# Keys and values of two groups projected by one 512-column pass, over three PSUM banks

## The reference

```python
q = rms_norm((ln(x) @ Wq.T).reshape(B, 64, 16, 128)); q = rope(q, itok)
kv_in = concat([ctx, ln(x)], axis=1)
k = rope(rms_norm(kv_in @ Wk.T), pos);  v = kv_in @ Wv.T          # 4 key/value heads, 4 queries each
x = x + tanh(g_xattn) * (softmax(q k^T / sqrt(128)) v) @ Wo.T
y = ln(x)
top = top_k(softmax(y @ w_router), 2)                            # 8 experts
x = x + tanh(g_ffn) * (2.5 * routed(y, top) + shared(y))
```

## Time and profile before

| | |
|---|---|
| median of 3 runs | 1232.29 us (1231.39 to 1232.36) |
| the profiled execution, its own time | 1230.35 us |
| its span | 1228.5 us |
| busy in the span | PE 1201.1, PEld 1115.2, DVE 1036.2, POOL 938.4, ACT 903.3 us |
| MATMUL records of `keys_values`, 256 wide | 1488 |
| MATMUL records of `queries`, 512 wide | 744 |

### The profile page before, as it was taken

How to read it: one execution, slowest core, us unless ns; L and a number is a source line. 1 busy time by engine, 2 the same in 40 slices (tenths; PEclk the granted TensorE clock), 3 DMA queues, 4 the chain that set the end, 5 groups by cost and what they waited for, 6 DMA issues and landing times.

```text
span 1228.5 us, 31467 instructions
## 1 busy us (share of the span) xinstructions
PE 1201.1 (98%) x8765; PEld 1115.2 (91%) x8766; DVE 1036.2 (84%) x3014; ACT 903.3 (74%) x3774; POOL 938.4 (76%) x1124
## 2 busy tenths in 40 slices
PE   6899999999999999999999999999999999999899
PEld 3788999999999999999999999999999899999787
DVE  8788999999999999999999999988888677777434
ACT  7978788878887888788887888877777546666322
POOL 2788888888888888888888888888887425556664
PEclk9999999999999999999999999999999999999989
DMA  6634233322222223323333333222236536554575
GB/s 179 198 110 130 75 108 107 103 90 90 90 90 90 94 90 94 90 90 98 115 106 98 103 107 119 93 76 75 75 110 215 192 101 188 167 163 146 155 250 170
DMA packets 141079, 148.55 MB, mean 121 GB/s; under 512 B 13824, under 2 KB 124672, under 8 KB 140256
## 3 DMA queue, kind: packets, MB, share of 16 engines
q1 hardware_dynamic: 134544, 130.16, 35.1%
q0 software_dynamic: 6480, 17.77, 3.9%
HBM read 66.93 MB, written 80.76 MB: 120 GB/s over the span
## 4 chain that ended last, share of the span: by engine, by line
PE 92%; DVE 4%; ACT 3%; DMA 1%; issue 1%; SPq 0%; DVEq 0%; ACTq 0%
PE b_kv L1795 14%; PE b_q L1781 13%; PE b_o L1879 13%; PE b_sc L1853 9%; PE b_aT L1868 9%; PE b_pT L1861 5%; PE b_qT L1842 4%; PE b_q L2115 3%; PE b_kv L2115 3%; PE b_kT L1838 2%; PE b_q L2175 1%; PE b_kT L2175 1%; PE b_o L2175 1%; PE b_kv L2175 1%; PE b_aT L2132 1%; PE b_pT L2132 1%
## 5 line engine op out<-in xcount | busy, mean ns | idle before, releaser
L1795 PE MATMUL b_kv<-w_group,kv_in_hi 128*128 128x256 f32 x992 | 205.0, 305 | 0.0
L778 POOL TENSOR_TENSOR q_rot<-q_rot,q_sin 128x512 f32<-128x512 f32 x128 | 176.6, 1380 | 7.3 <-DVE q_sin L1327 2.4
L984 ACT ACTIVATE probs<-b_sc,neg_max 128x128 f32<-128x128 f32 x512 | 180.2, 369 | 2.5 <-DVE neg_max L1337 2.1
L774 POOL TENSOR_TENSOR qk_r<-qk_me,minus_half 128x6 f32<-128x6 f32 x128 | 171.8, 1342 | 10.1
L1795 PEld LDWEIGHTS b_kv<-w_group,kv_in_hi 128*128 128x128 f32 x992 | 161.4, 190 | 7.3 <-issue 0.4
L1781 PE MATMUL b_q<-w_group,kv_in_hi 128*128 128x512 f32 x496 | 164.8, 413 | 0.4 <-DVE q_sin L1327 0.4
L1879 PE MATMUL b_o<-wo_hi,aT_hi 128*128 128x256 f32 x480 | 143.6, 299 | 0.3 <-DVE aT_lo L1351 0.3
L1853 PE MATMUL b_sc<-kT,qT 128*128 128x128 f32 x1024 | 136.4, 276 | 6.1 <-ACT qT L973 4.4
L781 POOL TENSOR_TENSOR q_rot<-q_rot,qk_r 128x512 f32<-128x512 f32 x128 | 133.5, 1043 | 10.0
L1795 PE MATMUL b_kv<-w_group,kv_in_lo 128*128 128x256 f32 x496 | 139.7, 282 | 0.0
L1868 PE MATMUL b_aT<-pT,v 128*128 128x256 f32 x512 | 133.9, 384 | 0.0
(11 more groups left out here) (332 smaller groups left out, 3978.2 us busy)
## 6 DMA issues: line engine op xcount, KB each, us to landing
xs_scratch<-zeros SPq DMA_DIRECT2D x34, 1032.0 KB, 6.2
s_in<-xs_scratch SPq DMA_DIRECT2D x71, 129.0 KB, 2.2
yT_scratch<-yT SPq DMA_DIRECT2D x32, 256.0 KB, 2.0
yS<-yT_scratch SPq DMA_DIRECT2D x32, 256.0 KB, 4.1
routed<-ys_scratch SPq DMA_DIRECT2D x32, 256.0 KB, 4.1
w_hi_all<-w_scratch SPq DMA_DIRECT2D x3, 1536.0 KB, 12.7
x_in<-in_x SPq DMA_DIRECT2D x32, 128.0 KB, 2.4
ctx_raw<-in_ctxT SPq DMA_DIRECT2D x32, 128.0 KB, 2.6
```

What stands on the lines that cost most here:

```text
L774: nc.gpsimd.tensor_tensor(qk_r[g % 2][:], qk_me[:], minus_half[:, 0:REP + NB], ALU.pow).then_inc(r_ready, 1)
L778: nc.gpsimd.tensor_tensor(q_rot[g % 2][:], q_rot[g % 2][:], q_sin[g % 2][:], ALU.add) \
L984: last = nc.scalar.activation(probs[:, j, :], b_sc[:, j * P:(j + 1) * P], ACT.Exp, bias=neg_max[g % 2][:, j:j + 1], accum_out=row_sum[g % ...
L1795: last = nc.tensor.matmul(b_kv[:, s * 2 * HD:(s + 1) * 2 * HD], kv_in[p][a][:, c, 2 * s:2 * s + 2, :], wkv_of(b, c)[:, g % KVH, :], start= ...
```

## The change

`b_kv` becomes one tensor of three banks. The first sequence's half (s=0) of groups 0 and 1 goes to bank 0, that of groups 2 and 3 to bank 2, and the second sequence's half (s=1) of either two groups to bank 1. `keys_values_of_two` computes one such half for two groups at once: six matmuls of 512 columns, s=0 in the odd units (for the two groups that start three units later), s=1 in the even ones. It takes the place of `keys_values` from unit 5 on. The bank for that comes from: transposed queries and probabilities in one bank `b_qp`; transposed keys into `b_sc`, where the scores follow; normed x, tokens and ranks into `b_aT`, where the attended values follow; the router's logits into `b_qp`. DVE reads ranks, x and tokens ahead of `turn_keys`; it turns the second sequence's keys first, and signals each sequence. ACT's tanh stands behind the key squares of g=0 instead of at the end of g=3. The banks of the later stages are renamed to fit.

```diff
-        b_q, b_kv, b_qT, b_kT, b_sc, b_pT, b_aT, b_o = [
-            bank(n) for n in ("b_q", "b_kv", "b_qT", "b_kT", "b_sc", "b_pT", "b_aT", "b_o")]
+        b_q = bank("b_q")
+        b_kv = ctx.enter_context(nc.psum_tensor("b_kv", [P, 3 * 512], F32))
+        b_qp, b_sc, b_aT, b_o = [bank(n) for n in ("b_qp", "b_sc", "b_aT", "b_o")]
...
+        def kv_bank(g, s):
+            return 1 if s == 1 else 2 * (g % KVH // 2)
...
+        def yT_rows(t):
+            return b_qp[:, D:2 * D] if isinstance(t, int) and t == TILES - 1 else b_aT[:, 0:D]
...
                 need(act, kv_done, n + 1)
-                kv = b_kv[:].rearrange("p (b w n) -> p b w n", b=NB, w=2)
+                if g % 2 == 1:
+                    need(act, k_turned, 2 * n)
+                kv = kv_of(g)
...
+                    if g == 0 and not first:
+                        lead_tanh(t - 2)
                     if not (first and u == 0):
                         queries_out(n, g)
...
-                    if g == 3 and not (end or first and p == 0):
-                        lead_tanh(t - 1)
...
-                for b in range(NB):
+                kv = kv_of(g)
+                for b in (1, 0):
...
-                last.then_inc(k_turned, 1)
+                      .then_inc(k_turned, 1)
...
                     score_max(n, g)
+                    if g == 0 and not first:
+                        read_ranks(t - 2, b_aT)
+                    if g == 1 and not end:
+                        normed_lo(t + 1, 1 - p)
+                    if g == 2 and not (first and p == 0):
+                        tokens_lo(t - 1, 1 - p)
...
                     if not (end and g == 3):
                         turn_keys(n + 1, g + 1, p1)
-                    if g == 0 and not first:
-                        read_ranks(t - 2)
...
-                    if g == 1 and not end:
-                        normed_lo(t + 1, 1 - p)
...
+            def keys_values_of_two(n, g, s, t, p):
+
+                if s == 0:
+                    need(pe, k_turned, 2 * (n - 2))
+                    if g == 0:
+                        need(pe, ctx_lo, t)
+                        need(pe, x_lo, t)
+                else:
+                    need(pe, k_turned, 2 * n - 1)
+                o = 512 * kv_bank(g, s)
+                for c in range(DC):
+                    for a, b in PASSES:
+                        last = nc.tensor.matmul(b_kv[:, o:o + 512].rearrange("p (g n) -> p g n", g=2),
+                                                kv_in[p][a][:, c, 2 * s:2 * s + 2, :],
+                                                wkv_of(b, c)[:, g:g + 2, :],
+                                                start=(c == 0 and (a, b) == PASSES[0]),
+                                                stop=(c == DC - 1 and (a, b) == PASSES[-1]))
+                if s == 1:
+                    last.then_inc(kv_done, 2)
...
             def heads_T(n, g):
+                need(pe, exp_done, n)
                 need(pe, k_ready, n + 1)
...
-                    last = nc.tensor.transpose(b_kT[:, s * P:(s + 1) * P], k_rot[g % 2][:, s, :], ident[:])
+                    last = nc.tensor.transpose(b_sc[:, s * P:(s + 1) * P], k_rot[g % 2][:, s, :], ident[:])
...
-                    last = nc.tensor.transpose(b_qT[:, h * P:(h + 1) * P], q_rot[g % 2][:, h, :], ident[:])
+                    last = nc.tensor.transpose(b_qp[:, h * P:(h + 1) * P], q_rot[g % 2][:, h, :], ident[:])
...
-                need(pe, exp_done, n)
                 need(pe, k_out, n + 1)
...
-                    if g == 2 and not end:
-                        need(pe, x_lo, t + 1)
-                    if g == 3 and not (first and p == 0):
-                        need(pe, yT_lo, t)
...
-                    if g == 1 and not first:
-                        need(pe, rk_read, t - 1)
...
                     if g == 3 and not (first and p == 0):
+                        need(pe, pT_out, n)
                         router(t - 1)
...
+                    if g == 0 and not first:
+                        need(pe, rk_read, t - 1)
+                    if g == 1 and not end:
+                        need(pe, x_lo, t + 1)
+                    if g == 2 and not (first and p == 0):
+                        need(pe, yT_lo, t)
                     if not (first and u < 1):
                         attend(n - 1, g - 1)
...
-                    elif not (end and g >= 2):
+                    elif first and u < 6:
                         keys_values(n + 2, g + 2, t2, p2)
+                    elif g % 2 == 0 and not (end and g == 2):
+                        keys_values_of_two(n + 2, (g + 2) % KVH, 1, t2, p2)
+                    if g % 2 == 1 and not (first and u < 5 or end):
+                        keys_values_of_two(n + 3, (g + 3) % KVH, 0, t + 1, 1 - p)
```

More of the change, by code:

```diff
@@ L319, in bank, with kv_of @@
             return ctx.enter_context(nc.psum_tensor(name, [P, 512], F32))
-        b_q, b_kv, b_qT, b_kT, b_sc, b_pT, b_aT, b_o = [
-            bank(n) for n in ("b_q", "b_kv", "b_qT", "b_kT", "b_sc", "b_pT", "b_aT", "b_o")]
-        b_count = b_table = b_kT
-        b_angle = (b_sc, b_pT, b_aT)
-        b_sg, b_shT, b_sT, b_sy = [b_q, b_kv], [b_qT, b_sc], [b_kT, b_o], [b_aT, b_pT]
-        b_early = (b_q, b_kv, b_pT, b_aT), (b_qT, b_sc, b_pT, b_aT)
-        b_gate, b_up, b_down = (b_q, b_kv), (b_kT, b_o), (b_sc, b_qT, b_aT, b_pT)
+        b_q = bank("b_q")
+        b_kv = ctx.enter_context(nc.psum_tensor("b_kv", [P, 3 * 512], F32))
+        b_qp, b_sc, b_aT, b_o = [bank(n) for n in ("b_qp", "b_sc", "b_aT", "b_o")]
+        b_kv0, b_kv1, b_kv2 = [b_kv[:, 512 * n:512 * (n + 1)] for n in range(3)]
+        b_count = b_table = b_qp
+        b_angle = (b_sc, b_qp, b_o)
+        b_sg, b_shT, b_sT, b_sy = [b_q, b_kv0], [b_kv1, b_sc], [b_qp, b_o], [b_aT, b_kv2]
+        b_early = (b_q, b_kv0, b_kv2, b_aT), (b_kv1, b_sc, b_kv2, b_aT)
+        b_gate, b_up, b_down = (b_q, b_kv0), (b_qp, b_o), (b_sc, b_kv1, b_aT, b_kv2)
+        def kv_bank(g, s):
+            return 1 if s == 1 else 2 * (g % KVH // 2)
+        def kv_of(g):
+            both = b_kv[:].rearrange("p (k j w n) -> p k j w n", k=3, j=2, w=2)[:, :, g % 2, :, :]
+            return both[:, 0:2, :, :] if g % KVH < 2 else both[:, 2:0:-1, :, :]
+        def yT_rows(t):
+            return b_qp[:, D:2 * D] if isinstance(t, int) and t == TILES - 1 else b_aT[:, 0:D]
         def sem(name):
@@ L785, in key_sum @@
             def key_sum(n, g):
-                need(pool, k_turned, n + 1)
+                need(pool, k_turned, 2 * (n + 1))
                 nc.gpsimd.tensor_tensor(k_rot[g % 2][:], k_rot[g % 2][:], k_sin[g % 2][:], ALU.add) \
@@ L1431, in rows_of_tokens, with read_ranks @@
                 nc.vector.tensor_copy(row_i[p][:], row_f[:]).then_inc(row_ready, 1)
-            def read_ranks(t):
+            def read_ranks(t, bank):
                 need(dve, rk_done, t + 1)
-                nc.vector.tensor_tensor(ranked[:], pick[:], b_kT[:, D:D + E].unsqueeze(1).to_broadcast([P, TOPK, E]),
+                nc.vector.tensor_tensor(ranked[:], pick[:], bank[:, D:D + E].unsqueeze(1).to_broadcast([P, TOPK, E]),
                                         ALU.mult).then_inc(rk_read, 1)
@@ L1608, in _ @@
             attended_lo(4 * TILES - 1, 3)
-            read_ranks(T2)
+            read_ranks(T2, b_qp)
             hidden_lo(0)
@@ L1632, in _ @@
             hidden(4)
-            read_ranks(T1)
+            read_ranks(T1, b_qp)
             rows_of_tokens(T1, 1)
@@ L1787, in keys_values @@
             def keys_values(n, g, t, p):
-                need(pe, k_turned, n)
+                need(pe, k_turned, 2 * n)
                 if g % KVH == 0:
@@ L1792, in keys_values @@
                 for s in range(NB):
+                    o = 512 * kv_bank(g, s) + 2 * HD * (g % 2)
                     for c in range(DC):
                         for a, b in PASSES:
-                            last = nc.tensor.matmul(b_kv[:, s * 2 * HD:(s + 1) * 2 * HD],
+                            last = nc.tensor.matmul(b_kv[:, o:o + 2 * HD],
                                                     kv_in[p][a][:, c, 2 * s:2 * s + 2, :],
@@ L1813, in first_keys_values @@
             def first_keys_values(g):
-                need(pe, k_turned, g)
+                need(pe, k_turned, 2 * g)
                 pe.wait_ge(ctx_hi, 1)
                 for s in range(NB):
+                    o = 512 * kv_bank(g, s) + 2 * HD * (g % 2)
                     for c in range(DC):
-                        last = nc.tensor.matmul(b_kv[:, s * 2 * HD:(s + 1) * 2 * HD],
+                        last = nc.tensor.matmul(b_kv[:, o:o + 2 * HD],
                                                 kv_first[:, c, 2 * s:2 * s + 2, :],
@@ L1860, in probs_T @@
                 for j in range(REP):
-                    last = nc.tensor.transpose(b_pT[:, j * P:(j + 1) * P], probs[:, j, :], ident[:])
```

(15 more changed lines are left out.)

41 lines of the change are left out of this document (19 added, 22 removed).

## The result

The changed kernel takes 1250.26 us, median of 4 runs (1247.49 to 1252.84), against 1232.16 of the kernel before: a ratio of 1.0149, interval 1.0133 to 1.0165. That is 1.5% slower, where I had forecast 0.44% faster and had put slower at 0.09. The profiled execution took 1247.49 us, its span is 1245.7 (before: 1228.5).

What follows compares the result with a forecast made beforehand. PE, nearly alone, was taken to bound 827 us of attention, about 115 units. Savings of 4.6 + 0.8 = 5.4 us off the profiled 1230.35 gave 1224.95, or 1226.9 us against the median; range 1222.5 to 1231.5.

Steps and rivals of the forecast that it cites:

- The 512-wide blocks: PE's keys and values: six 512-column matmuls for twelve save 0.04 us a unit, 4.6 us over 115 units (0 to 6.9).
- Waits that move: DVE's readers ahead of `attend`: 0.74 us to spare in g=1, 0.4 for the new block in g=0; no cost.
- Shared banks: Waits from banks used twice, such as transposed keys in `b_sc` (1.5 us to spare): all hidden, cost nothing.
- The tanh: ACT's tanh behind g=0's key squares: shorter stalls in a loop turn's first unit, 0.8 us saved (0 to 2.6).
- Width costs its columns: Rival, chance 0.14: each 512-wide matmul takes 2 × 0.119 us, PE saves nothing, only the tanh's 0.8 us remains; 1231.5 us.
- DVE late at `attend`: Rival, chance 0.09: readers asked for ahead of `attend` have 0.7 us of cover; DVE later than that stalls PE; 1235 us.

Runs made afterwards that it cites:

- the eighth experiment: Changed kernel with POOL's second scatter moved from g=2 to g=3, and `seen` and the second normalising's statistics behind the turned keys: 1231.66 us, ratio 0.9997.
- experiment 2: Changed kernel with each 512-wide matmul made two of 256 columns, same banks, order and waits: 1250.47 us, ratio 1.0151.
- experiment 5: Kernel before with only the tokens' reader (`tokens_lo`, g=2) moved ahead of the turned keys: 1241.17 us, ratio 1.0072.
- experiment 10: Kernel before with only POOL's second scatter moved to g=3 and the wait for its transfer later: 1229.08 us, ratio 0.9998.
- the ninth: The eighth experiment's kernel with each 512-wide matmul of keys and values as two of 256 columns, same banks and order: 1230.65 us, ratio 1.0008.
- experiment 4: Kernel before with only the tanh moved behind the key squares of g=0: 1231.87 us, ratio 1.0005.
- experiment 1: Kernel before with only DVE's three readers (ranks and `seen`, normed x, tokens) moved ahead of the turned keys: 1245.92 us, ratio 1.0117.
- (6): Kernel before with only the ranks' reader (`read_ranks`, g=0: `ranked`, then `seen`) moved ahead of the turned keys: 1233.11 us, ratio 1.0011.

## Why the prediction was wrong

- **The 512-wide blocks:** right in mechanism and size for the block itself. 36 ns a unit measured (1614 to 1578) for the 40 forecast. Wrong as a term of the sum: in the eighth experiment the projection, behind the transposes that follow the block, runs at its slower pitch in 59 of 100 units, and two thirds are lost again; in the changed kernel itself DVE sets the pace and all of it is lost (experiment 2).
- **The Trainium skill** ("TensorE: Matmul & The Clock Gate", Back-to-back issue gap) has 2.5 ns beside the columns, and gives this as the gap of isolated matmuls, which the prediction did not say. Beside the columns at 2.4 GHz, the runs here have 113.4 - 106.7 = 6.7 or 117.8 - 106.7 = 11.1 for 256 columns. The formula gave too small a saving for the block (15 ns for 36), and has no second level.
- **Waits that move** is the step that failed. I looked at each moved reader from PE's side only: does PE get to `attend` after it. That was right (0.23 behind the queries, no wait hit). I then wrote "POOL is not late for PE by this" and stopped. The prediction's own times had the second sequence's keys done at 510.4 and POOL free at 510.20, and I priced these 0.2 at nothing. POOL's key sum was late where the wait shows (25 times, all in g=1, 0.43 on average; in g=2 0.31 in experiment 5's unit), and what came of it is not that PE waited for POOL, but that POOL's next operations slid over DVE's. I had priced lateness of DVE at 0.1 us for 0.1 us a tile, had the place wrong (`attend`) and no term at all for DVE operations growing by 0.15 to 0.49 us. I even had the row: `seen` ending with POOL's L781, and took it as a fact about `seen` alone. The same test on `wg_lo` would have shown it ending 0.48 behind the sine table, with 0.36 us of cover behind it for the copy of the keys.
- The Trainium skill ("SBUF — State Buffer", Who interferes with whom) calls this pair of ports an exclusive lock held for a whole instruction. The runs agree: with the sine table out of the way the same subtraction takes 600 ns (experiment 10) in place of 1805. What I failed to do is to carry the rule to each DVE operation with two SBUF inputs behind the moved ones.
- **Shared banks:** as good as free, as forecast (the eighth keeps them all, at 0.9997, and the ninth, without the width, at 1.0008).
- **The tanh:** forecast 0.8 us, measured nothing (experiment 4). The stall passes to the next unit.
- **The rivals.** *Width costs its columns* is wrong for the block, and by the projection's pitch close to right for the kernel. *DVE late at `attend`* had the engine and the sign, not the place: the waits are the scores' for the key copy in g=3, in the unit behind the moved reader's, and in g=1 that of the transposes of the normed `x`; in g=3 0.36 us of cover decide it, not 0.7.
- Two costs I did not price at all: the additional half block in unit 5, where DVE sets the pace (8.45 to 9.84 in the eighth, 1.4 us; 10.29 in the changed kernel), and the wait for the scatter at tile 30 (2.2).

Of the 18 us: the order of DVE's work makes 14.8 by itself (experiment 1), the tokens' reader 9.2 of it (5), the ranks' 1.2 (6); the normed reader was not run alone, so the last 4.4 may be its or what the three do together. The additional half block makes 1.4. Left open: the rest of some 2 us; why the output projection has two pitches and what brings the slower one (the wide block does in the eighth against the ninth, never in g=1 there, and the tenth has it without a wide block); and the changed kernel's runs, which lie at 1247.5 to 1247.9 and at 1252.6 to 1252.8 with nothing between. One place where such a step could come from is the last unit of tile 30, 9.53, 9.92, 9.99 and 10.77 long in the profiles of four kernels with early readers (8.15 with the tokens' alone), but no two profiles of one kernel show it. The step is as large as 5 us, so what is said above of 2 or 3 us between two of these kernels is not certain.

## What to carry to other kernels

When work moves on one engine, follow whom it makes late, and then what that engine does at the same time as the first one's later work: two engines that share a port are a schedule of their own, and a shift of 0.3 to 0.5 us there cost 0.3 us a tile in the unit behind here, with no wait between the two in the program. Before a reorder, list the operations whose span ends at a fixed distance behind another engine's; each is a wait that no semaphore shows, and its cover has to be priced like one. Where such a collision is found, moving the other engine's work to where it is idle (one scatter, 16.5 us) can be cheaper than moving your own back; look at what it meets in its new place, too (experiment 10).
